# Key and value products first, query products behind them, and the first attention group's gathers in the same block of the program

## The reference, cut to what matters

```python
hn = _batch_norm(h, bn1_g, bn1_b)
Q = (hn @ Wq).reshape(n, H, HD)
K = (hn @ Wk).reshape(n, H, HD)
V = (hn @ Wv).reshape(n, H, HD)
score = jnp.einsum('ehd,ehd->eh', K[src], Q[dst]) / np.sqrt(HD)
score = jnp.clip(score, -5.0, 5.0)
...
m = V[src] * a[:, :, None]
wV = jax.ops.segment_sum(m, dst, num_segments=n).reshape(n, DIM)
```

## Time and profile before

| | |
|---|---|
| Time, median of 3 runs | 1287.67 us (1286.55 to 1288.09) |
| The profiled execution's own time | 1286.43 us |
| Its span, first to last instruction | 1284.1 us |
| Busy share of the span: PE, DVE, ACT, POOL | 77%, 68%, 41%, 47% |
| Mean granted PE clock, of full speed | 0.815 |

### The profile page before, as it was taken

One profiled execution on the slowest core, in us unless ns is written; L12 is line 12 of the kernel. 1 busy time (PEld: TensorE's weight loads), 2 busy tenths in 40 slices (PEclk: granted clock), 3 DMA queues, 4 the chain that ended last, 5 costly groups with the idle time before them and its releaser, 6 DMA issues. The chain is left out here.

```text
span 1284.1 us, 18303 instructions
## 1 busy us (share of the span) xinstructions
PE 987.3 (77%) x6064; PEld 622.0 (48%) x6064; DVE 875.0 (68%) x2176; ACT 529.1 (41%) x1067; POOL 609.0 (47%) x770
## 2 busy tenths in 40 slices
PE   2289989999999999896746666666666666648997
PEld 1168855655655556353624444444444444325654
DVE  2879965764544466556557888888788888865443
ACT  1189932211111111111456656666666566633210
POOL 3100059959267230320167777777777777740000
PEclk9985579999999999898865567777776766758998
DMA  6100044000000000000453333333333333327111
GB/s 147 44 2 1 2 128 128 1 18 1 1 9 1 17 16 18 21 1 1 115 153 113 111 107 115 112 108 110 115 107 111 107 115 111 109 69 171 50 49 29
DMA packets 52558, 88.03 MB, mean 69 GB/s; under 512 B 12721, under 2 KB 38678, under 8 KB 52215
## 3 DMA queue, kind: packets, MB, share of 16 engines
q0 software_dynamic: 19888, 52.52, 14.0%
q1 hardware_dynamic: 30086, 32.72, 9.3%
q10 hardware_dynamic: 2492, 1.61, 0.5%
HBM read 71.05 MB, written 15.76 MB: 68 GB/s over the span
## 5 line engine op out<-in xcount | busy, mean ns | idle before, releaser
L1674 POOL DMA_INDIRECT counts_all<-kv_d,early_buf x391 | 377.2, 965 | 148.6 <-issue 146.3
L1062 PE MATMUL bank<-counts_all,parts 125*128 125x500 f16 (+2 forms) x1750 | 342.2, 355 | 6.6 <-PEq L602 3.5
L1062 PEld LDWEIGHTS bank<-counts_all,parts 125*128 125x128 f16 x1750 | 160.3, 98 | 175.4 <-issue 9.8
L1858 PE MATMUL bank<-counts_all 125*128 125x128 f16 x1218 | 128.8, 283 | 44.0 <-ACT counts_all L1960 43.6
L1858 PEld LDWEIGHTS bank<-counts_all 125*128 125x128 f16 x1218 | 106.8, 130 | 85.1 <-ACT counts_all L1960 82.7
L1873 PE MATMUL bank<-counts_all,parts 128*128 128x272 f16 x609 | 128.3, 366 | 5.4 <-DVE counts_all L1723 5.4
L1769 DVE TENSOR_TENSOR counts_all<-counts_all,bank 128x512 f32<-128x512 f32 x104 | 71.2, 685 | 80.2 <-DMA counts_all<-kv_d,early_buf 79.8
L1847 PE MATMUL bank<-rel_rows,ident_h 104*128 104x512 f16 x104 | 55.8, 536 | 83.7 <-ACT away L1950 60.7
L717 PE MATMUL bank<-parts 128*125 128x125 f16 x625 | 102.7, 324 | 11.8 <-DVE parts L636 11.8
L1950 ACT ACTIVATE away<-bank,lane_bias 125x512 f16<-125x512 f32 x170 | 109.0, 680 | 1.1 <-PE bank L1847 0.7
L1715 DVE TENSOR_TENSOR parts<-bank,early_buf 128x1012 f16<-128x1012 f32 (+1 forms) x104 | 105.6, 1016 | 0.0
(11 more groups left out here) (338 smaller groups left out, 1455.9 us busy)
## 6 DMA issues: line engine op xcount, KB each, us to landing
counts_d<-counts_all SPq DMA_DIRECT2D x1, 6835.9 KB
counts_all<-kv_d,early_buf POOLq DMA_INDIRECT x391
counts_all<-counts_d SPq DMA_DIRECT2D x1, 4785.2 KB
counts_all<-kv_d SPq DMA_DIRECT2D x25, 128.0 KB, 2.2
kv_d<-counts_all SPq DMA_DIRECT2D x6, 448.0 KB
counts_all<-counts_d SPq DMA_DIRECT2D x3, 683.6 KB
q_d<-counts_all SPq DMA_DIRECT2D x1, 1562.5 KB
x<-in_x SPq DMA_DIRECT2D x6, 250.0 KB
```

The costliest lines, as they stand in the source:

```text
L1062: last = T.matmul(agg_ps[p][:, 0:w], pin[:, s, part, :], counts[:, s, bass.ds(b * BLK, w)], start=(s + part == 0), stop=(s + part == NT))
L1674: G.indirect_dma_start(out=out_rows, out_offset=None, in_=table_d, in_offset=bass.IndirectOffsetOnAxis(ap=index, axis=0)).then_inc(signal, 16)
L1858: last = T.matmul(pick_ps[n % DEEP][:, k * C:(k + 1) * C], ohT[n % DEEP][:, tile - GTILES[n][0], k, :], Q[:, tile, part, :], start=(tile = ...
```

## The change

In the block of the products, PE first forms keys and values of all 25 tiles and then all 25 queries; `qkv_done` becomes `kv_done` and `q_done`. The normalized features of all tiles are kept for that (`hn_T` is now one buffer over memory that the attention block uses later), so `norm` no longer waits for a buffer. ACT copies keys and values as before and then all queries' high halves; DVE only subtracts. POOL, when all of `kv_d` has been written, loads the flags, branches, and issues the four gathers of group 0 there; in the attention block its loop begins with group 1. The two blocks of the program, and the barrier between them, stay.

```diff
-                hn_T = [carve([C, BLK]) for _ in range(2)]
+                hn_T = parts_all[0][:, :, :, :].rearrange("p t h c -> p (t h c)").bitcast(fp32)
...
                         G.memset(acc[:, :, :], 0.0)
+                        pool.wait_ge(att_in, 32)
+                        pool.wait_ge(kv_out_done[0], 32 * (NBLK // 2 + 1))
+                        pool.wait_ge(kv_out_done[1], 32 * (NBLK // 2))
+                        wide = windows_spanned(ET.Pool)
+                        with pool.If(wide <= 1):
+                            for k in range(GRP):
+                                G.indirect_dma_start(out=kv[:, 0, k, :], out_offset=None, in_=kv_d,
+                                                     in_offset=bass.IndirectOffsetOnAxis(ap=att_src[:, EDGES_OF[k]:EDGES_OF[k] + 1], axis=0)
+                                                     ).then_inc(kv_in[0], 16)
...
                                 if n >= 3:
                                     pe.wait_ge(kv_copied, n - 2)
-                                    pe.wait_ge(q_copied, n - 2)
-                                T.matmul(kv_ps[n % 3][0:TILE, 0:2 * C], hn, wkvq[:, 0:2, :].rearrange("p w c -> p (w c)"),
-                                         start=True, stop=True)
-                                T.matmul(ps[5 + n % 3][0:TILE, 0:C], hn, wkvq[:, 2, :], start=True, stop=True).then_inc(qkv_done, 1)
+                                T.matmul(kv_ps[n % 3][0:TILE, 0:2 * C], hn_T[:, (t0 + j) * TILE:(t0 + j + 1) * TILE],
+                                         wkvq[:, 0:2, :].rearrange("p w c -> p (w c)"), start=True, stop=True).then_inc(kv_done, 1)
+                        for tile in range(NT):
+                            if tile >= 3:
+                                pe.wait_ge(q_copied, tile - 2)
+                            T.matmul(ps[5 + tile % 3][0:TILE, 0:C], hn_T[:, tile * TILE:(tile + 1) * TILE], wkvq[:, 2, :],
+                                     start=True, stop=True).then_inc(q_done, 1)
...
+                        for tile in range(NT):
+                            dve.wait_ge(q_high, tile + 1)
+                            V.tensor_tensor(Q[:, tile, 1, :], ps[5 + tile % 3][0:TILE, 0:C], Q[:, tile, 0, :],
                                             ALU.subtract).then_inc(q_copied, 1)
...
-                            if i >= 2:
-                                act.wait_ge(qkv_done, first_tile[i - 1])
...
-                                act.wait_ge(qkv_done, n + 1)
+                                act.wait_ge(kv_done, n + 1)
                                 S.copy(kv_out[i % 2][:, j, :], kv_ps[n % 3][0:TILE, 0:2 * C]).then_inc(kv_copied, 1)
+                        for tile in range(NT):
+                            act.wait_ge(q_done, tile + 1)
+                            S.copy(Q[:, tile, 0, :], ps[5 + tile % 3][0:TILE, 0:C]).then_inc(q_high, 1)
...
                     with pool.If(wide <= 1):
-                        for g in range(NG):
+                        for g in range(1, NG):
                             if g >= RING:
                                 pool.wait_ge(va_ready, g - RING + 1)
```

More of the change, by code:

```diff
@@ L1496, in build, with windows_spanned @@
             gen_added = sem("gen_added")
+            def windows_spanned(engine):
+                return load_registers(nc, engine, att_flags[0:1, 0:4], NT)[1]
             arena_at[0] = arena_mid
@@ L1507, in build @@
                 hn_ready = sem("hn_ready")
-                qkv_done = sem("qkv_done")
+                kv_done = sem("kv_done")
+                q_done = sem("q_done")
                 kv_copied = sem("kv_copied")
@@ L1552, in _ @@
                                 n = first_tile[i] + j
-                                hn = hn_T[i % 2][:, j * TILE:(j + 1) * TILE]
                                 if n >= 3:
                                     pe.wait_ge(kv_copied, n - 2)
-                                    pe.wait_ge(q_copied, n - 2)
-                                T.matmul(kv_ps[n % 3][0:TILE, 0:2 * C], hn, wkvq[:, 0:2, :].rearrange("p w c -> p (w c)"),
-                                         start=True, stop=True)
-                                T.matmul(ps[5 + n % 3][0:TILE, 0:C], hn, wkvq[:, 2, :], start=True, stop=True).then_inc(qkv_done, 1)
+                                T.matmul(kv_ps[n % 3][0:TILE, 0:2 * C], hn_T[:, (t0 + j) * TILE:(t0 + j + 1) * TILE],
[5 more added lines that the diff above has]
+                                     start=True, stop=True).then_inc(q_done, 1)
                     @block.vector
@@ L1577, in _ @@
                         st.run(V.tensor_copy(qidx[:, :], qidx_f[:, :]))
-                        def q_low(n, tile):
-                            dve.wait_ge(q_high, n + 1)
-                            V.tensor_tensor(Q[:, tile, 1, :], ps[5 + n % 3][0:TILE, 0:C], Q[:, tile, 0, :],
+                        for tile in range(NT):
+                            dve.wait_ge(q_high, tile + 1)
+                            V.tensor_tensor(Q[:, tile, 1, :], ps[5 + tile % 3][0:TILE, 0:C], Q[:, tile, 0, :],
                                             ALU.subtract).then_inc(q_copied, 1)
[L1584 to L1592, removed]
                     @block.scalar
@@ L1601, in norm @@
                             act.wait_ge(x2_turned, min(i, NBLK) + NBLK if i >= 2 else NBLK + 1)
-                            if i >= 2:
-                                act.wait_ge(qkv_done, first_tile[i - 1])
-                            w = order[i][2]
-                            S.activation(hn_T[i % 2][:, 0:w], ps[2 + i % 2][:, 0:w], ACT.Identity,
+                            w, d0 = order[i][2], order[i][1]
+                            S.activation(hn_T[:, d0:d0 + w], ps[2 + i % 2][:, 0:w], ACT.Identity,
                                          scale=bcol[:, 4:5], bias=bcol[:, 5:6]).then_inc(hn_ready, 1)
@@ L1624, in build @@
             a_ps = [ps[7][:, 32 * i:32 * i + 32].rearrange("p (k h) -> p k h", h=HEADS) for i in range(2)]
-            def windows_spanned(engine):
-                return load_registers(nc, engine, att_flags[0:1, 0:4], NT)[1]
             TURN_AT = {LAST_OF[t] + 6: t for t in range(NT) if LAST_OF[t] + 7 < NG}
```

## The result

The change makes the kernel slower, by some 0.4%. Over nine runs of each, the median is 1292.35 us (1289.2 to 1301.34) against 1286.93 us before (1285.81 to 1289.15). The ratio is 1.0039, with a 95% interval of 1.002 to 1.0058, so 2.6 to 7.5 us. The forecast was 1294.0 us, from a sum of 6.7 us more.

The account below looks back on a forecast made before the run. POOL's gathers bound attention, ACT's stream setting when gather 12 begins. Landing at 636.3 + 3.0 + 4.94 + 4.1 = 648.4, barrier 6.7 us later; 1287.67 + 6.7 = 1294.4, given as 1294.0, range 1290.0 to 1296.3.

Parts of the forecast that it names:

- the forecast's own case: Barrier after the products' block 5.5 to 8 us later, nothing back from the early gathers; chance 0.60.
- the first rival: At the products' block's end, POOL's DRAIN does not wait for gathers: barrier 2.6 us later, 1290.3 us; chance 0.18.
- Keys and values first, 5.3 us earlier: Products' block: last landing of keys and values at 636.3 instead of 641.6, 5.3 us earlier.
- Queries hidden: End of products' block: queries take 0.38 us each, 9.5 in all, beside POOL's longer new work, nearly 6 us to spare.
- POOL's new work: Ahead of the barrier: 3.0 us to first gather, 4.94 for four, then the DRAIN; 12 us behind the landing.
- The DRAIN, "I take 4.1": POOL's DRAIN behind the early gathers at the products' block's end: 4.1 us, as at the attention block's end.
- Nothing back from the early gathers: Attention block: gathers worth 5.0 us taken out gain nothing; POOL's wait before gather 12 grows from 1.16 to about 6.1.
- the second rival: Attention block: the early gathers pay back all 5.0 us behind the barrier, giving +1.7, 1289.4 us; chance 0.11.
- the DRAIN that doesn't wait: End of products' block: POOL's DRAIN waits for no gathers, barrier only 2.6 us later, 1290.3 us; chance 0.18.
- the early gathers that pay: Attention block loses 5.0 us behind the barrier because of the early gathers: 1289.4 us; chance 0.11.
- the later landing: Products' block: key and value transfers, closer together, land later than 3.6 us; for 2 us of landing 1296.5; chance 0.11.

Follow-up runs that it names:

- n0_none: The changed kernel without the four early gathers, all gathers back in the attention block: median 1287.52 us, ratio 0.9997 against the kernel before.
- beside: The changed kernel plus a 1.6 MB write by SP to `q_d` beside the four early gathers: 1298.15 us (one run).
- clears: The changed kernel with POOL clearing four buffers in place of the early gathers, all gathers in the attention block: 1286.49 us (one run).
- n11_early: The changed kernel with all eleven gathers of groups 0 to 2 ahead of the barrier instead of four: 1299.77 us, ratio 1.0105 against before.
- exp_early: The changed kernel with a one-column exponential at the start of ACT's attention stream, loading its table early: 1288.72 us (one run).

## Why the prediction was right

The mechanism held in each of its steps. Two sizes were off, and together they made the forecast 2.6 us too long. So the barrier came 4.1 us later, which is neither the "5.5 to 8 us" of the forecast's own case nor the 2.6 us of the first rival. That the time still lies near 1294.0 is owed in part to scatter (below).

- *Keys and values first, 5.3 us earlier:* the copies ended 5.4 earlier (20.1 against 25.5), with the forecast wait for landings on ACT. From the last copy to the landing it took 3.2 us and not 3.6, so the landing came 5.8 earlier. This term was 0.5 too small, which is within the scatter of single traces. That the copies agree to 0.1 us is luck in part: the first five tiles took 8.4 us (627.48 + 0.80 less 619.87) and not the 7.8 of the forecast (620.2 less 612.45), and the last block ended 4.8 us behind the one two before it (640.0 less 635.25) and not 5.1.
- *Queries hidden:* 0.39 us a tile against 0.38, and 3.3 us to spare ahead of POOL's end instead of "nearly 6". That they would hold the barrier where it was without that cover was shown by n0_none, to within 0.7 us.
- *POOL's new work:* 3.0 us from the first load of the flags to the first gather (643.3 to 646.26) and 4.95 for the four, as forecast.
- *The DRAIN, "I take 4.1":* this term was mis-sized; it took 2.0. That it waits for the gathers' data was shown, by beside against the change, with the gathers' packets in both, and by clears. Taking its size from the attention block's end was wrong. The last section shows the part in which the two differ.
- *Nothing back from the early gathers:* the distance from the barrier to gather 12 stayed at 17.9 us with four and with eleven early gathers, and was 17.8 with none (n0_none). POOL's wait was 6.76 against "about 6.1", since its first gather came 2.7 us after the flags instead of 3.0 and was 0.24 shorter (0.95 against 1.19). With a barrier only 4.1 us later this step decided the sign, as the second rival says: with all 5.0 back, gather 12 would have come 0.9 us sooner than before.

The sum is 6.7 - 2.1 - 0.5 = 4.1 us, and the traces show 4.1 for both the barrier and gather 12. The medians differ by 5.4 us, which the interval (2.6 to 7.5) doesn't tell from 4.1. The 1.3 us between the two bring the time nearer to the forecast, and no step of the prediction accounts for them. The stretch behind gather 12 differs between profiled executions by more than the 1.3 us that are left: from gather 12 to the end of the last gather are 484.8 us in the change (671.30 to 1156.06), 482.0 before, and 483.6 in n0_none, with the same code there.

Of the rivals, the DRAIN that doesn't wait fell with beside, the early gathers that pay with n0_none, n11_early and exp_early, and the later landing with the row of SP: closer together, the transfers landed sooner, not later.

## What to carry to other kernels

A wait that an engine shows is not yet what its work is late by: DVE waited 8.91 us for gathers, and the result behind it was set by ACT, which from its first distances to the exponential ran without a gap; look for the operand that comes last at the next step, and ask whether a gain there meets a stream without gaps. What is moved ahead of a barrier is paid by every engine, with the DRAIN behind it, so it must end by the time the block would end anyway. And where a stage's end has two parts, shortening one is worth something only once the other ends as early.

## What the runs showed of the hardware that was not expected

**A DRAIN behind gathers has two parts.** The trace's memory traffic, GB/s in 40 slices, between 650 and 655 in the change (slices of 0.125 us):

```profile
GB/s 33 0 0 0 0 197 295 66 360 99 33 0 0 0 0 131 197 328 164 164 66 0 0 0 0 0 0 0 0 0 0 0 0 0 0 0 0 0 0 0
```

The same in the kernel before, between 1140 and 1150 (slices of 0.25 us), at the end of the attention block:

```profile
GB/s 197 229 49 0 33 262 180 49 0 0 229 262 33 0 0 0 0 0 0 0 0 0 0 0 0 0 0 0 0 0 0 0 0 0 0 0 0 0 0 0
```

Only the gathers' queue moved anything in these two stretches. In both places the traffic goes on for 1.4 us after the last gather's recorded end: until 652.6 (recorded end 651.21), and until 1143.25 (1141.81); the queue's last packets, 0.1 us later, carry too little to show in these rows. The Trainium skill, Perfetto Trace Analysis, section "DMA Instruction — SWDGE (GPSIMD)", puts the recorded end where the descriptors are written and not where the data has moved, and this agrees. But the DRAIN ended 0.6 us after the last traffic behind four gathers (653.2), and 2.7 us after it behind 391 (1145.9). This second part is what made the row of the attention block's end too long a price. It was there in the changed kernel too: at its attention block's end the DRAIN ended at 1159.9, 3.9 us behind the last gather. Behind eleven gathers the DRAIN took 2.3 us in all (n11_early, 654.4 against 652.12). What grows with the number of gathers, or with what else ran before, stays open.

**A load of registers took twice as long at the start of a large transfer.** The two loads of POOL in beside, in ns and with their starts:

```profile
L145 POOLq TENSOR_LOAD <-early_buf x2: 983/1618/2254, 639.5 to 654.0; - x2
```

The first load, at 639.5, took 2.25 us; SP began to issue its write at 639.45. The second took 0.98, although the write still ran beside it (until about 656.5); in the change the two took 0.97 and 1.16. So by these rows it isn't the traffic as such that slows a load. PE's loads of the flags fit this: in all ten traces they start 0.3 to 0.6 us behind the start of SP's issue of the queries' write and take 2.7 to 3.1 us, while the other engines' loads behind the same barrier start ahead of it and take 0.9 to 1.2. What in the start of a write would do it stays open, and no run moved that write. In beside the slow load made the first gather come 4.1 us after the flags rather than 3.0, so it is in that kernel's 37.1 too.
